# Attention in two halves of the batches, with the next layers' first stages inside the second half

## The reference

```python
x = layernorm(x + attention(x))                 # 32 query heads, 8 key/value heads of 64, rotary, causal
x = layernorm(x + expert(x, fside[b], ctx[b]))  # smooth-quantized: gate/up (512 -> 2*256), silu(gate)*up, down (256 -> 512)
x = layernorm(x + ffn(x))                       # signs of weights: relu(x @ sign(Wup).T * up_s) @ sign(Wdn).T * down_s * out_s

def smooth_quant_linear(x, w):
    s  = sqrt(max|x| per column / max|w| per column)
    xs, ws = x / s, w * s
    x_scale, w_scale = max|xs| per row / 127, max|ws| per row / 127
    return round(xs / x_scale) @ round(ws / w_scale).T * x_scale * w_scale.T
```

## Time and profile before

| | us |
|---|---|
| median of three runs | 1488.9 (1485.17 to 1490.07) |
| the profiled execution's own time | 1488.69 |
| its span, first to last instruction | 1486.9 |
| PE busy | 1303.3 |
| DVE busy | 1068.3 |
| ACT busy | 907.5 |
| POOL busy | 534.9 |
| mean granted PE clock | 0.953 of full speed |

### The profile page before, as it was taken

The page is one execution under the profiler, slowest core; times in us unless marked ns, Lnnn a source line. Parts: engine busy times, 40 slices in busy tenths (PEclk is TensorE's granted clock), DMA queues, the critical chain, the costliest instruction groups (busy, mean ns, idle before and its releaser), DMA issues. The chain is left out here.

```text
span 1486.9 us, 26399 instructions
## 1 busy us (share of the span) xinstructions
PE 1303.3 (88%) x7112; PEld 1087.8 (73%) x7112; DVE 1068.3 (72%) x2572; ACT 907.5 (61%) x2137; POOL 534.9 (36%) x436
## 2 busy tenths in 40 slices
PE   2799999999999999999999999998622589899996
PEld 2578888878878887887888888887511367677775
DVE  3688878877878887887887888887848755855322
ACT  2576677666667766776666677666335465555332
POOL 3233244233434332452342343332012143635443
PEclk9899999999999999999999999999955699999999
DMA  4341122222122211212211122211054110110000
GB/s 168 115 121 36 37 55 68 55 54 57 36 51 75 51 38 51 57 47 62 70 36 37 50 68 55 56 37 36 15 219 155 43 43 29 43 43 36 8 29 29
DMA packets 47818, 88.07 MB, mean 59 GB/s; under 512 B 10960, under 2 KB 13008, under 8 KB 45648
## 3 DMA queue, kind: packets, MB, share of 16 engines
q1 hardware_dynamic: 47696, 86.82, 20.0%
HBM read 40.64 MB, written 4.19 MB: 30 GB/s over the span
## 5 line engine op out<-in xcount | busy, mean ns | idle before, releaser
L453 ACT ACTIVATE probs<-probs,neg_max 128x128 f32<-128x128 f32 (+3 forms) x512 | 285.5, 560 | 185.9 <-DVE neg_max L580 185.5
L653 DVE TENSOR_TENSOR pT_lo<-ps_t,pT_hi 128x512 fp32r<-128x512 f32 (+1 forms) x384 | 218.1, 595 | 83.5 <-ACT pT_hi L508 63.8
L724 PE MATMUL ps_s<-k_st,q_st 128*128 128x256 f32 (+2 forms) x1024 | 221.3, 338 | 27.7 <-DVE neg_max L580 25.8
L580 DVE CUSTOM_DVE_ANT_0 probs<-ps_s,mask 128x128 f32<-128x128 f32 (+3 forms) x512 | 228.3, 481 | 3.2 <-PE ps_s L724 2.7
L724 PEld LDWEIGHTS ps_s<-k_st,q_st 128*128 128x128 f32 x1024 | 158.7, 190 | 45.9 <-DVE neg_max L580 32.9
L376 POOL TENSOR_TENSOR o_lo<-o_sum,o_hi 128x512 fp32r<-128x512 f32 x64 | 81.9, 1280 | 291.0 <-ACT o_hi L468 291.0
L508 ACT ACTIVATE pT_hi<-ps_t 128x512 fp32r<-128x512 f32 (+1 forms) x384 | 174.6, 528 | 6.1 <-PE ps_t L769 3.1
L769 PE MATMUL ps_t<-ident,probs 128*128 128x128 f32 x1280 | 163.4, 275 | 14.9 <-ACT probs L453 14.9
L781 PE MATMUL ps_o<-pT_hi,v_st 128*128 128x256 f32 (+2 forms) x512 | 168.5, 340 | 0.0
L769 PEld LDWEIGHTS ps_t<-ident,probs 128*128 128x128 f32 x1280 | 143.4, 141 | 20.1 <-ACT probs L453 10.3
L781 PE MATMUL ps_o<-pT_lo,v_st 128*128 128x256 f32 (+2 forms) x512 | 155.7, 326 | 0.0
(11 more groups left out here) (194 smaller groups left out, 2936.3 us busy)
## 6 DMA issues: line engine op xcount, KB each, us to landing
q_st<-q_tmp SPq DMA_DIRECT2D x512, 64.0 KB, 2.0
k_st<-k_st SPq DMA_DIRECT2D x64, 128.0 KB, 2.3
raw<-in_wq_t SPq DMA_DIRECT2D x16, 256.0 KB, 3.1
y<-in_x_t SPq DMA_DIRECT2D x4, 1024.0 KB, 10.3
y<-in_x SPq DMA_DIRECT2D x4, 1024.0 KB, 5.9
raw<-in_wo_t SPq DMA_DIRECT2D x16, 256.0 KB, 2.7
w_gu<-in_fside_t SPq DMA_DIRECT2D x4, 1024.0 KB, 4.8
stage<-in_up_t SPq DMA_DIRECT2D x4, 1024.0 KB, 10.7
```

The source lines that it names most:

```text
L453: act.activation(probs[:, h % 2, SO[i]:SO[i] + SW[i]], probs[:, h % 2, SO[i]:SO[i] + SW[i]], ACT.Exp, bias=neg_max[:, h % 2, i:i + 1], sca ...
L580: dve.tensor_tensor_reduce(out=probs[:, h % 2, SO[i]:SO[i] + SW[i]], in0=ps_s[:, i % 2, 0:SW[i]], in1=mask[:, L - SW[i]:L], scale=-SCALE, ...
L653: dve.tensor_tensor(pT_lo[:, d, :], ps_t[:, k, 0:P * w].rearrange("p (w c) -> p w c", c=P), f32(pT_hi[:, d, :]), ALU.subtract).then_inc(p_ ...
L724: i = pe.matmul(dst, a, c, start=(j == 0), stop=(j == len(terms) - 1))
```

## The change

What it does:

- *One program.* `build` now holds everything in one block; tiles of the attention and of the later layers are laid over each other in memory (the feed-forward weights' 16 tiles `ffn_t`, up and down of one tile together, go where attention tiles were, once these are no longer used). `xT_hi`/`xT_lo` hold two batches instead of four and serve as `x2T` later.
- *Halves.* 16 passes instead of 8: first all eight key/value heads for batches 0 and 1, then for batches 2 and 3. The rolled loop covers passes 1 to 5; 6 to 15 are written out. Each key/value head's weights are loaded and split twice.
- *Room.* `ps_t` has two banks instead of three; the third transpose group goes behind the output product. The freed bank `pc` serves the gate/up and down layers of batches 0 and 1, one bank instead of two or three.
- *Moves between engines.* The key rotation goes from DVE to POOL (ACT now copies keys and values out of PSUM), the repeated reciprocals go from DVE to POOL, the low parts of x for batches 2 and 3 too.
- *Stages in the second half.* After each head (slots 0 to 63) the engines run the stages that `PLACED` gives to that slot: norms of batches 0 and 1, gate/up of 0 and 1, down, second norm and transposes of 0, weight maxima, and loads and signs of the first six weight tiles. Big DVE stages are split into two.
- *The rest.* From slot 64 on, ticks as before: batch 3's output products, norms of 2 and 3, gate/up of 2 and 3, down of 1 to 3, ten signs, and 64 up and 64 down tiles.

The diff, cut to its core:

```diff
-T_BANKS = [[(0, 0), (0, 1), (0, 2), (0, 3)], [(1, 1), (1, 2), (1, 3), (3, 3)], [(2, 2), (2, 3)]]
+T_BLOCKS = [[(0, 0), (0, 1), (0, 2), (0, 3)], [(1, 1), (1, 2), (1, 3), (3, 3)], [(2, 2), (2, 3)]]
+HALF = 2
+STEPS = B // HALF * HKV
+SLOTS = STEPS // 2 * HALF * G
+PERIOD = 2 * HT
+PLACED = [
+    (0, "A", 0, "0 dve wmax0\n1 dve wmax1\n3 sp w"),
+    (1, "N", 0, N_STAGES),
+    (5, "A", 0, A_SLOW),
+    (17, "N", 1, N_STAGES),
+    (18, "B", 0, "0 sp wT\n3 dve wmax\n5 sp w"),
+    (28, "B", 0, B_SLOW),
+    (37, "A", 1, "0 sp wT\n4 dve wmax0\n5 dve wmax1\n7 sp w"),
+    (41, "A", 1, A_SLOW),
+    (59, "B", 0, X2T),
...
+    (SLOTS, "N", 2, N_STAGES),
+    (SLOTS + 1, "T", 0, T_STAGES),
+    (SLOTS + 5, "A", 2, A_FAST),
+    (SLOTS + 3, "B", 1, B_FAST),
+    (SLOTS + 24, "B", 1, X2T),
+    (SLOTS + 12, "N", 3, N_STAGES),
...
+PLACED += [(at, "S", h, "0 sp load") for h, at in enumerate([55, 59, 59, 59, 60, 60] + [63] * 5 + [64] * 5)]
+PLACED += [(at, "S", h, "0 act sign") for h, at in enumerate([57, 61, 61, 62, 62, 63] + [SLOTS + 2 * h - 8 for h in range(6, HT)])]
...
-        ps_t = pb("ps_t", [P, 3, L])
+        ps_t = pb("ps_t", [P, 2, L])
+        pc = pb("pc", [P, L])
...
+        def steps(eng, body):
+            body(0, 0)
+            with eng.Fori(1, HKV - 2) as g:
+                body(g, 0)
+            body(HKV - 2, 0)
+            body(HKV - 1, 0)
+            for g in range(HKV, STEPS):
+                body(g, 1)
...
+        def rope_k(eng, u):
+            eng.wait_ge(v_copied, u + 1)
+            eng.tensor_tensor(k_tmp[0:HF, 1, :], k_tmp[HF:HD, 0, :], sin_k[HF:HD, :], ALU.mult).then_inc(k_prod, 1)
+            eng.tensor_tensor(k_tmp[HF:HD, 1, :], k_tmp[0:HF, 0, :], sin_k[0:HF, :], ALU.mult).then_inc(k_prod, 1)
+            eng.wait_ge(k_prod, u * 3 + 2)
+            eng.tensor_tensor(k_tmp[0:HD, 0, :], k_tmp[0:HD, 0, :], cos_sb[0:HD, :], ALU.mult).then_inc(k_prod, 1)
...
+            def repeat_r(g, b, p):
+                u = g * HALF + b
+                pool.wait_ge(r_done, u * G + (2 * p + 2))
...
+                pool.tensor_copy(r_rep[:, :, :, :],
+                                 r_inv[:, :, p, :].unsqueeze(3).to_broadcast([P, QT, 2, HD])).then_inc(r_repd, 1)
...
+            def transpose_probs(n, h, k):
+                wait(pe, p_lo, n * 3 + (k - 1))
+                pe.wait_ge(exped, n * 4 + 4)
...
+                        transpose_probs(n, h, 0)
+                        transpose_probs(n, h, 1)
+                        if more:
+                            scores(*ahead, 0)
+                            scores(*ahead, 1)
...
+                        transpose_probs(n, h, 2)
+                        if more:
+                            scores(*ahead, 2)
+                            scores(*ahead, 3)
+                        if half == 1:
+                            later("pe", slot(g, b, h))
```

More of the change, by code:

```diff
@@ new lines @@
+"""
+B_SLOW = """
+    0 dve colmax
+    1 pe colx
+    1 dve ratio
+    1 act root
+    2 dve reps
+    3 pe rows
+    3 act roww
+    3 dve xs
+    4 pool ws0
+    5 pool ws1
+    4 dve xabs
+    5 act xround0 xround1
+    6 dve wabs xq
+    7 act wround0 wround1
+    7 pe xT
+    7 act xqT
+    8 dve wq
+    9 pe wT
+    9 act wqT
+    10 pe wrow
+    10 act wrow
+    11 pe prod0
+    11 dve prod0
+    11 pool add0
+    12 pe prod1
+    12 dve prod1
+    12 pool add1
+    13 pe prod2
+    13 dve prod2
+    13 pool add2
+    14 pe prod3
+    14 dve prod3
+    14 pool add3
+    16 dve var20
+    17 dve var21
+    17 act std2
+    18 dve y20
+    19 dve y21
@@ new lines @@
+"""
+B_FAST = """
+    0 dve colmax
+    2 pe colx
+    2 dve ratio
+    3 act root
+    4 dve reps
+    5 pe rows
+    5 act roww
+    5 pool ws0
+    6 pool ws1
+    6 dve xs xabs
+    7 act xround0 xround1
+    8 dve wabs xq
+    9 pe xT
+    9 act wround0 wround1
+    9 act xqT
+    10 dve wq
+    11 pe wT
+    11 act wqT
+    12 pe wrow
+    12 act wrow
+    13 pe prod0
+    13 dve prod0
+    13 pool add0
+    14 pe prod1
+    14 dve prod1
+    14 pool add1
+    15 pe prod2
+    15 dve prod2
+    15 pool add2
+    16 pe prod3
+    16 dve prod3
+    16 pool add3
+    17 dve var20 var21
+    18 act std2
+    19 dve y20 y21
@@ new lines, in x_later, with slot, run @@
+            return [at[g, b, h]] if isinstance(g, int) and (g, b, h) in at else []
+        def steps(eng, body):
[6 more added lines that the diff above has]
+                body(g, 1)
+        def slot(g, b, h):
+            return ((g - HKV) * HALF + b) * G + h
+        def run(eng, feed, later):
+            for tick in range(SLOTS, TICKS):
+                if feed is not None:
+                    feed(*divmod(tick - SLOTS, PERIOD))
+                later(eng, tick)
@@ new lines, in f, with later @@
+            def f(b, name):
+                for t in range(QT):
+                    n = b * QT + t
+                    pool.wait_ge(dn_read, n + 1)
+                    pool.tensor_tensor(y[:, n, :], y[:, n, :], pr_f[:, t, :], ALU.add).then_inc(f_added, 1)
+            def later(eng, tick):
+                for chain, b, name in at_tick(eng, tick):
+                    {"A": a, "B": b_, "F": f}[chain](b, name)
+            steps(pool, body)
+            low_o(U - 1, 1, 1)
+            run("pool", feed, later)
@@ L714, in _ @@
-            for i in range(QT):
-                dve.wait_ge(tail_full, i + 1)
-                t = (B - 1) * QT + i
-                dve.tensor_tensor(y[:, t, :], y[:, t, :], tail_banks[i], ALU.add)
+            normalize(STEPS - 1, HALF - 1, 1)
+            run("dve", feed, later)
         @block.tensor
@@ L1187, in spread @@
+            def spread(dst, src, n):
                 for k in range(n):
```

1713 lines of the change are left out of this document (959 added, 754 removed), and 28 rows, old and new, of the table PLAN.

## The result

The changed kernel takes 1483.2 us (median of five runs, 1480.5 to 1484.4) against 1488.8 us (1485.2 to 1490.1) for the kernel before: a ratio of 0.996, 95% interval 0.9947 to 0.9974. It is faster by 0.4%, where 4.3% was forecast; 1483.2 lies outside the range of 1392 to 1476. The profiled execution took 1484.37 us for a span of 1482.6.

What follows compares the result with a forecast made beforehand. TensorE was taken as the bound in attention. Last reciprocal at 1060.8 + 5.6 + 39.8 = 1106.2 us, 3.3 to the first up tile, 300.1 feed-forward, 13.7 tail: span 1423.3, time 1425 us, 4.3% less; range 1392 to 1476.

Steps and rivals of the forecast that it cites:

- (1) Order of attention: Attention loop: sixteen two-batch passes replace eight four-batch passes, with one loop turn fewer; +5.6 us.
- (2) Weights twice: Attention: 40 more weight splits on GpSimd and copies on ScalarE, hidden in slack; 0, up to 24 us.
- (4) two banks: Attention: third transpose of a head waits for the first low part, but the wait is covered; 0, bounds 0 and 32.
- (3) GpSimd takes over: Attention: key rotation and repeated reciprocals go from VectorE to GpSimd; 0, as TensorE is full in all units.
- the slower rival: Attention: GpSimd's queue delivers repeated reciprocals late and holds TensorE 2.3 us per unit; about 1499 us, chance 0.09.
- (5) Insertion: Second half of attention: norm, gate/up, down and other stages placed after heads lengthen it by 40 us, bounds 20 and 96.
- VectorE's term: Stages in the second half: most slots fit VectorE's slack, six are over by about 1 us; +6 us.
- TensorE term: Stages in the second half: 19.8 us of TensorE work, all on the path, plus 4 us for semaphores.
- ScalarE term: Stages in the second half: 16 table loads of 1.28 us, half on the path, other work in slack; +10 us.
- (6) The hole goes: Between attention and feed-forward: TensorE's mostly idle stretch vanishes; first up tile 3.3 us after the last head's reciprocal.
- (7) Feed-forward: Feed-forward: 5.6 us of batch 3's output products plus 8 us of new stalls, in batch 0's period; +13.6, bounds 5.6 and 30.
- The "dearer" case: Second half of attention: the heads' chain takes VectorE's added work in full, insertion about 85 us; 1445 to 1484, chance 0.24.

Runs made afterwards that it cites:

- b3: Changed kernel with three transposition banks instead of two in the first half of attention, all transpositions ahead of the output products: first half 508.5 us instead of 509.3.
- p_base: Changed kernel with GpSimd's own attention work of the second half cut to 8 columns, inserted stages whole: second half 563.1 us against 587.3.
- stt: Changed kernel with VectorE's tensor_scalars of the stages written as scalar_tensor_tensor with two SBUF operands: 1489.9 us, ratio 1.0008 to the kernel before.
- early4: Changed kernel with VectorE's stage moved ahead of the query rotation in slots 4, 12, ... 52 only: 1463.4 us, ratio 0.9832 to the kernel before.

## Why the prediction failed, point by point

*(1) Order of attention, +5.6.* Right within some 2 us: 1009.3 us without the insertion, an estimate, against 1007.0.

*(2) Weights twice, (4) two banks: 0.* Both right. First-half passes of 63.5 us (62.8 forecast, below the 64 that would have broken it) and 0.8 us for the third bank (`b3`). "So the wait is covered" is borne out by the 14.3 and 14.2 us.

*(3) GpSimd takes over: 0.* Right for what was asked: GpSimd's copy takes 0.61 us, inside the bounds of 0.46 and 1.3, and PE never waits for the repeated reciprocals, so the slower rival has nothing for it. But the question was asked of one side only. "POOL's operations show 1.28 us beside a DVE that is 81% busy" is true of most of them after as before, but says nothing of what VectorE loses. GpSimd itself loses little, 1.44 to 1.60 us in the few places of the second half where VectorE was in first.

*(5) Insertion, +40: the step that failed.* It cost 87 (estimate above), and that is 47 of the 59 us. What failed in it are VectorE's term, put at 6 us, and a term that wasn't there, GpSimd holding VectorE. Term by term:

| term | forecast | measured, alone |
|---|---|---|
| TensorE's work | 19.8 + 4 | 2.7 to 3.9 for 13 us of it, with the clock moving against it |
| VectorE's work | 6 | 24.8 |
| ScalarE, of it tables | 10, 10 | 17.0, 6.1 |
| VectorE held by GpSimd | not in the sum | 24.2 (`p_base`) |
| not settled | | about 16 |

The terms don't add up exactly, since each was measured with the others present; with all stages thin and GpSimd narrow 71.6 us are gone.

Whether the TensorE term ("on a bound engine, so all of it on the path") was too large stays open: the 2.7 and 3.9 us are differences at different clocks, and TensorE's idle time moved by only 2 to 3 us. The VectorE term was too small by a factor of four, because slack was counted per head and on the mean. In a head whose TensorE list has nothing between second scores and third transposition there is no slack at all behind VectorE, however idle it is elsewhere. The row that said so was at hand: ScalarE's 101 waits for the maxima, which the text quoted as a warning and then priced at six slots of 1 us. The ScalarE term was near in its tables (half of the loads forecast, a third measured) and left out the rest of its work. By the 2.66 us a switch of the Trainium skill (ScalarE: Activation LUTs, "What ACT_TABLE_LOAD costs") it would have been 21, an estimate; the loads show 1283 ns and cost 6.1 in all, so the trace's price was the better one.

The missing term is the block, and it is the largest single mistake. The added VectorE work was priced at its durations in the hole, where GpSimd was busy 18.7 of 111.5 us; it was moved to where GpSimd is busy half the time (290 of 587 us). Most VectorE operations of the attention have an operand in PSUM, so the rows chosen from before showed no held one. The trace of before has them all the same. First the low part of x, which reads both its inputs from SBUF, in the attention from 61.0 us on; then the cast that takes 661 ns in the hole, here in the feed-forward, where GpSimd is busy 132 of 287 us (by shape):

```profile
L621 DVE TENSOR_TENSOR xT_lo<-y,xT_hi 128x512 fp32r<-128x512 f32 x4 | 3.6, 945 | 0.0
...
L1499 DVE TENSOR_SCALAR xq_b<-av 128x1024 bf16<-128x1024 f32 x3 | 4.0, 1323 | 1.7 <-ACT av L1309 1.7
```

The first has a median of 681 ns over the whole run and reaches 1791. So the price could have been read before the change was made. The Trainium skill ("SBUF — State Buffer", "Who interferes with whom") states the rule: VectorE's copies, casts and tensor_scalars in their fast mode, and its operations with two SBUF inputs (these against a GpSimd operation that reads SBUF), use ports that GpSimd uses too; whichever is first has them for its whole instruction, and the other blocks. The runs agree with it in kind: `stt` for the two-input form, the unchanged 1211 ns of the reduction, and the 0.69 us of the low part. What the rule for one instruction doesn't say is that VectorE can miss its turn between two GpSimd instructions: in three places it was held to the end of a run of three, at most others of one. The rule spoke against the change and should have stood among the rivals.

The clock is a share of these costs, not one beside them. In slot 4 it is at the lower of its levels, 1.2 GHz, after TensorE has stood still for 4.08 us. Where the list of products is unchanged, TensorE's busy time shows the share: 510.6 us in the changed kernel, 500.8 in `early4` (granted clock 0.99 instead of 0.97) and 501.9 in `p_base` (0.98). So about 10 of `early4`'s 20.6 us and 9 of `p_base`'s 24.2 are products that run faster again, an estimate, and the rest is shorter waiting.

*(6) The hole goes.* Right: the first up tile comes 4.7 us after the last reciprocal (3.3 forecast), with no slice below 7 tenths.

*(7) Feed-forward, +13.6.* The right sign, but a third short: +20.0 with the tail (320.2 against 300.2). Its first two periods (answers to the earlier trace rows):

```profile
1162.40:1250.30 87.90, 79.92 (x387) 61.58 (x388) 62.67 (x107) 54.32 (x81) 35.17 (x29) 0.96 0.22 78
1250.30:1334.10 83.80, 75.63 (x372) 57.49 (x372) 51.20 (x82) 44.37 (x69) 38.60 (x33) 0.98 0.08 26
```

The first is 87.9 us where 95 was forecast, 5.7 more than before, as much as the 5.6 us of output products; but the second grew by 7.4 (from 76.4), the third by 4.2 (72.7 from 68.5) and what follows by 2.7, where the forecast had put nothing. In the second, TensorE waits 3.9 us for VectorE's cast `xq` (L1436), which takes 2.2 us at 1279.63 beside a GpSimd operation where it takes 1.2 elsewhere, and 2.7 us for the cast `xq_b` (L1487). No run was made on it, so how much of the growth this is stays open.

*The rivals.* The "dearer" case, 1445 to 1484, is where the time fell, at its very end, and second-half passes of 74.6 us crossed the 73 named for it. Its mechanism, VectorE's work in series, is a quarter of the truth, and that its insertion of about 85 us lies beside the measured 87 is luck: its own terms, 76 in place of 6, give 40 + 70 = 110. The prediction also says that table loads at 2.66 us a switch land in this case; 11 us more give 1436, which is inside the forecast's own 1405 to 1445.

## What to carry to other kernels

Before work is moved from an idle stretch into a busy one, price it by what its engine meets there: which of its operations another engine's operations hold up, and whether the head or tile it lands in has anything for the bound engine to do meanwhile. A chain through a half-idle engine has no room at its tight place. To price work on TensorE by cutting it, look at its busy and idle time and its granted clock apart: the length alone can hide most of it. When a schedule is written out by hand, look at the cost slot by slot: moving one stage in seven of 64 slots gained 1.3%, moving it in all gained nothing.

## What the runs showed of the hardware

VectorE's tensor_scalars and casts, and its forms with two operands in SBUF, are held while GpSimd runs, sometimes to the end of a whole run of operations: 8 columns took 3.47 us for two instructions, until the last of three back-to-back GpSimd operations of 1.27 us had ended; four columns took 3.20 us in one place and 0.70 in another. Their width doesn't matter. Elsewhere VectorE was let in after one GpSimd operation. Most of GpSimd's own operations stay at 1.26 to 1.30 us, but beside one of these that was in first they took 1.44 to 1.60. Reductions (1.21 us) and operations with an operand in PSUM (0.69) run at full speed beside GpSimd. 15 table loads of 1.28 us cost 6.1 us of the path, 0.4 us each, a third of their duration, from one execution.
